# Low-rank rows by plain transfers, shared-expert matmuls in pieces of 5, 1, 1 and 5 pairs, expert rows summed tile by tile

## The reference

```python
def holo_linear(x, basis, phase, amp):          # basis 32x256, phase and amp 256x32
    resonance = jnp.einsum('bli,hi->blh', x, basis)
    w = amp * jnp.cos(phase)
    return jnp.einsum('blh,oh->blo', resonance, w)
# attention: 16 heads of 16
q, k, v = (split_heads(holo_linear(x, ...)) for each)
attn = jax.nn.softmax(jnp.einsum('bhqd,bhkd->bhqk', q, k) * scale, axis=-1)
out = holo_linear(join_heads(attn @ v), basis_o, phase_o, amp_o)
# experts: F = 352, best 2 of 8 by softmax of x @ gate_w.T, weights normed and times 2.5
g = silu(x @ w_gate[e]) * (x @ w_up[e]);  y = sum_e combine[t, e] * (g @ w_down[e])
shared = silu(x @ sw_gate) * (x @ sw_up) @ sw_down        # hidden size 704
return x + out(xn) + y(xn) + shared(xn)
```

## Time and profile before

| | |
|---|---|
| median of 3 runs | 1045.18 us (1043.41 to 1047.68) |
| the profiled execution | 1047.09 us, its span 1045.2 us |
| mean granted TensorE clock | 0.927 of full speed |
| PE busy | 888.3 us, 85% of the span |
| DVE busy | 642.8 us, 62% |
| ACT busy | 563.8 us, 54% |
| POOL busy | 328.7 us, 31% |
| 16 DMA engines, SyncE's queue | 42.2% |

### The profile page before, as it was taken

How to read it: one execution, slowest core, us unless ns; L and a number is a source line. 1 busy time by engine, 2 the same in 40 slices (tenths; PEclk the granted TensorE clock), 3 DMA queues, 4 the chain that set the end, 5 groups by cost and what they waited for, 6 DMA issues and landing times.

```text
span 1045.2 us, 19238 instructions
## 1 busy us (share of the span) xinstructions
PE 888.3 (85%) x6423; PEld 620.9 (59%) x6424; DVE 642.8 (62%) x978; ACT 563.8 (54%) x892; POOL 328.7 (31%) x305
## 2 busy tenths in 40 slices
PE   5646999999999956887997996996997998799988
PEld 3426999999999922445444554553644644545546
DVE  7767744444444373864784784785785686487653
ACT  4746644444444433663664664665565566466573
POOL 2004622222222031161261253234235126127235
PEclk9955999999999955998998998999999899899999
DMA  9974555222222143544654664664564575545220
GB/s 318 375 232 159 169 157 140 72 71 70 70 70 70 46 135 117 151 125 137 169 157 135 161 174 125 173 186 119 154 192 135 140 194 142 134 138 154 66 84 21
DMA packets 91537, 147.34 MB, mean 141 GB/s; under 512 B 17348, under 2 KB 51660, under 8 KB 88652
## 3 DMA queue, kind: packets, MB, share of 16 engines
q1 hardware_dynamic: 84780, 128.58, 42.2%
q0 software_dynamic: 6480, 17.70, 6.3%
q10 hardware_dynamic: 208, 0.14, 0.0%
HBM read 86.58 MB, written 54.71 MB: 135 GB/s over the span
## 4 chain that ended last, share of the span: by engine, by line
PE 54%; DVE 16%; DMA 15%; issue 6%; ACT 4%; POOL 2%; SPq 2%; POOLq 0%; DVEq 0%; ACTq 0%
DVE top L1836 8%; DMA r_v<-low_rank_rows 8%; PE bank L1266 7%; PE s_pair L1248 7%; PE st_pair L1248 6%; PE s_pair L1325 6%; DMA low_rank_rows<-r_lo 5%; PE bank L1409 5%; PE bank L1373 5%; PE bank L1483 4%; PE st_pair L1397 4%; ACT prob L1040 2%; PE bank L1256 2%; PE bank L1231 2%; PE bank L1423 1%
## 5 line engine op out<-in xcount | busy, mean ns | idle before, releaser
L1836 DVE TENSOR_REDUCE top<-s_pair 128x2 f32<-128x1024 f32 x252 | 308.3, 1224 | 198.1 <-PE s_pair L1325 197.2
L1040 ACT ACTIVATE prob<-st_pair 128x1024 f32<-128x1024 f32 x256 | 262.5, 1025 | 143.0 <-PE st_pair L1397 138.5
L751 POOL DMA_INDIRECT xg<-xn_rows,token_of x71 | 81.2, 1144 | 223.4 <-PE bank L1231 168.2
L784 POOL DMA_INDIRECT y_b<-expert_rows,slot_of x64 | 61.5, 961 | 265.7 <-PE st_pair L1397 260.6
L1325 PE MATMUL s_pair<-k_rows,q_rows 48*128 48x512 f32 x504 | 122.2, 478 | 24.6 <-DVE top L1836 23.2
L1373 PE MATMUL bank<-xT_b,w_sh 64*128 64x512 f32 x960 | 134.5, 397 | 4.9 <-DVE h_f L1857 3.5
L1397 PE MATMUL st_pair<-q_rows,k_rows 50*128 50x512 f32 x512 | 113.4, 437 | 18.4 <-ACT prob L1040 11.2
L1409 PE MATMUL bank<-prob,v_ones 128*32 128x512 f32 x1024 | 127.4, 616 | 0.0
L1373 PEld LDWEIGHTS bank<-xT_b,w_sh 64*128 64x128 f32 x960 | 89.8, 185 | 33.9 <-DVE h_f L1857 13.1
L1325 PEld LDWEIGHTS s_pair<-k_rows,q_rows 48*128 48x128 f32 x504 | 51.0, 196 | 76.4 <-DVE top L1836 59.7
L1266 PE MATMUL bank<-w_exp,c_hT 128*128 (+1 forms) x639 | 94.2, 292 | 1.0 <-ACT c_y L965 1.0
(11 more groups left out here) (233 smaller groups left out, 1109.9 us busy)
## 6 DMA issues: line engine op xcount, KB each, us to landing
xT_b<-xn_T_split SPq DMA_DIRECT2D x14, 1024.0 KB, 7.1
qk_rows<-qk_hi SPq DMA_DIRECT2D x56, 256.0 KB
q_rows<-qk_rows SPq DMA_DIRECT2D x64, 192.0 KB
k_rows<-qk_rows SPq DMA_DIRECT2D x56, 192.0 KB
expert_rows<-c_y SPq DMA_DIRECT2D x71, 128.0 KB, 1.7
xn_T_split<-x_T SPq DMA_DIRECT2D x8, 1024.0 KB, 6.5
qk_rows<-qk_lo SPq DMA_DIRECT2D x28, 256.0 KB
x_all<-in_L_attn_x_dram SPq DMA_DIRECT2D x8, 512.0 KB, 8.1
```

The costliest lines, as they stand in the source:

```text
L751: pool.indirect_dma_start(xg[s % 4][:, :], None, xn_dram, bass.IndirectOffsetOnAxis(token_of[:, s:s + 1], 0)).then_inc(c_x[s % 4], 16)
L784: pool.indirect_dma_start(y_b[:, t, k, :], None, y_dram, bass.IndirectOffsetOnAxis(slot_of[:, k, of(b) * TPB + t:of(b) * TPB + t + 1], 0)) ...
L1040: act.activation(prob[n % 3][:, 2 * jp:2 * jp + 2, :].rearrange("p j l -> p (j l)"), st_pair[:, :], ACT.Exp, scale=HD ** -0.5).then_inc(a_ ...
L1836: dve.tensor_reduce(top[g % 2][:, :, jp, qt], score_pair(b, g, v)[:, :].rearrange("p (i k) -> p i k", i=2), AX_X, ALU.max).then_inc(d_max, 1)
```

## The change

- The rows of q, k and v come into one buffer `r_rows[b % 2]` (96 partitions, 3 x 512), twice, in place of `r_qk` and two `r_v`. `load_low_rank` issues three transfers of 32 partitions each, HI, HI, LO, without a repeated source, in place of four. The wait for `b_qk` is one batch looser. `r_in` counts 48 a batch.
- To make room `r_lo` is the buffer `ro`; before ScalarE writes `ro` it waits for the stores of `r_lo`. An unused tile goes.
- SyncE issues `load_xT(b + 2)` in group 2 behind `load_max` and `load_rows`.
- The units of the shared expert are cut at 0, 5, 6, 7, 12 (down: 0, 10, 14, 19, 31, 34). Step 1 has the first piece, step 2 the second, then the small work, then the third, step 3 the fourth; down's fifth stays at the next step 0. The swap of the halves, with its wait for `b_ha`, lies between the second and the third piece.
- GpSimd scales and adds a tile's two expert rows as soon as its gathers and the one place later in its order allow (`sum_y`), with two semaphores `y_in`; `scale_y` and `add_pair` go. `hidden_low(b, 5)` is written at the head of the next batch's loop, where it stood at the end of its own.

```diff
             def load_low_rank(b):
                 wait(sp, r_st, (b + 1) * 32)
-                wait(sp, b_qk, b * 4)
+                wait(sp, b_qk, (b - 1) * 4)
                 wait(sp, b_v, (b - 1) * 2)
-                for rows, n, part in ((slice(0, 2 * HARM), 2, HI), (slice(2 * HARM, 3 * HARM), 1, LO)):
-                    src = r_dram[part].rearrange("(c h) n l -> c h (n l)", c=1).to_broadcast([n, HARM, 3 * L])
-                    sp.dma_start(r_qk[rows, :, :].rearrange("p n l -> p (n l)").bitcast(F32), src[:, :, 0:2 * L]).then_inc(r_in, 16)
-                    sp.dma_start(r_v[b % 2][rows, :].bitcast(F32), src[:, :, 2 * L:3 * L]).then_inc(r_in, 16)
+                for c, part in enumerate((HI, HI, LO)):
+                    sp.dma_start(r_rows[b % 2][c * HARM:(c + 1) * HARM, :, :].bitcast(F32), r_dram[part]).then_inc(r_in, 16)
...
-                if g == 2 and there(b + 2):
-                    load_xT(b + 2)
...
                 if there(rb):
                     load_rows(rb, rg)
+                if g == 2 and there(b + 2):
+                    load_xT(b + 2)
...
+            def sum_y(b, t):
+                wait(pool, y_in[t % 2], (b * 2 + t // 2 + 1) * 32)
+                for k in range(2):
+                    pool.tensor_scalar(y_b[:, t, k, :], y_b[:, t, k, :], share[:, of(b) * TPB + t, k:k + 1], None, ALU.mult).then_inc(p_ys, 1)
+                wait(pool, p_ys, (b * TPB + t + 1) * 2)
+                pool.tensor_tensor(y_b[:, t, 0, :], y_b[:, t, 0, :], y_b[:, t, 1, :], ALU.add).then_inc(p_yy, 1)
...
                 wait(act, b_po, b * 2)
+                wait(act, r_st, min(b + 3, NB) * 32)
                 act.activation(ro[:, :], res_bank(b)[0:96, :], ACT.Copy).then_inc(a_res, 1)
...
-            PIECES = ((0, 6), (6, 8), (8, 12))
-            DOWN_PIECES = ((0, 14), (14, 22), (22, 31), (31, 34))
+            CUTS = (0, 5, 6, 7, 12)
+            DOWN_CUTS = (0, 10, 14, 19, 31, 34)
...
-                    if t % 4:
-                        piece(b, g, t)
+                    if t % 4 == 1:
+                        piece(b, g, t, 0)
+                    if t % 4 == 2:
+                        piece(b, g, t, 1)
+                        small(b, g, t)
+                        piece(b, g, t, 2)
+                    if t % 4 == 3:
+                        piece(b, g, t, 3)
```

The order on GpSimd in a batch:

```diff
             for b in range(NB):
+                if there(b - 1):
+                    hidden_low(b - 1, 5)
                 gather_at(b, 0, 0, 4)
                 gather_at(b, 1, 0, 6)
                 gather_at(b, 2, 1, 0)
+                sum_y(b, 0)
                 gather_at(b, 3, 1, 2)
                 if there(b - 1):
                     ao_low(b - 1, 1)
                 hidden_low(b, 0)
                 gather_at(b, 4, 1, 7)
+                sum_y(b, 1)
                 gather_at(b, 5, 2, 1)
                 gather_at(b, 6, 2, 3)
                 hidden_low(b, 2)
                 gather_at(b, 7, 2, 6)
-                for n in range(4):
-                    scale_y(b, n)
+                sum_y(b, 2)
                 hidden_low(b, 3)
-                for n in range(4, 8):
-                    scale_y(b, n)
+                sum_y(b, 3)
                 ao_low(b, 0)
-                add_pair(b)
                 hidden_low(b, 4)
                 add_y(b)
-                hidden_low(b, 5)
+            hidden_low(LAST, 5)
```

More of the change, by code:

```diff
@@ L221, in build_program @@
         w_sh = sb("w_sh", [P, 2, S_ALL], F32R, late)
-        r_qk = sb("r_qk", [96, 2, L], F32R, late)
-        r_v = [None, sb("r_v1", [96, L], F32R, late)]
+        r_rows = [None, sb("r_rows1", [96, 3, L], F32R, late)]
         r_hi = sb("r_hi", [96, L], F32R, late)
-        r_lo = sb("r_lo", [96, L], F32R, late)
         qk_hi = [sb(f"qk_hi{i}", [P, L], F32R, late) for i in range(2)]
@@ L242, in build_program @@
         ro = sb("ro", [96, L], F32R, late)
+        r_lo = ro
         ao_T = sb("ao_T", [P, 2, KT, L], F32R, late)
@@ L247, in build_program @@
         o_b = sb("o_b", [P, TPB, D], F32, late)
+        r_rows[0] = sb("r_rows0", [96, 3, L], F32R, late)
         q_rows[0] = sb("q_rows0", [P, 2, L], F32R, late)
         k_rows[0] = sb("k_rows0", [P, 2, L], F32R, late)
-        r_v[0] = sb("r_v0", [96, L], F32R, late)
         xT_b = sb("xT_b", [P, 2, KT, L], F32R, late)
@@ L313, in build_program @@
         ob_in = sem("ob_in")
-        y_in = sem("y_in")
+        y_in = [sem(f"y_in{i}") for i in range(2)]
         m_in = [sem(f"m_in{i}") for i in range(2)]
@@ L554, in load_first_values @@
                 for c, part in enumerate((HI, HI, LO)):
-                    sp.dma_start(r_v[0][c * HARM:(c + 1) * HARM, :].bitcast(F32), r_dram[part, :, 2, :]).then_inc(r_in, 16)
+                    sp.dma_start(r_rows[0][c * HARM:(c + 1) * HARM, 2, :].bitcast(F32), r_dram[part, :, 2, :]).then_inc(r_in, 16)
             def store_y(s, i):
@@ L603, in store_low_rank @@
             def store_low_rank(b):
-                wait(sp, r_in, b * 64 - 16)
+                wait(sp, r_in, b * 48)
                 wait(sp, a_r, b + 1)
@@ L1314, in project @@
                     wait(pe, a_mt, (b - 1) * NG + 3)
-                pe.matmul(m_bank[:, :], w_rows[:, which, half * P:(half + 1) * P], r_qk[:, which, :], start=True, stop=True).then_inc(b_qk, 1)
+                pe.matmul(m_bank[:, :], w_rows[:, which, half * P:(half + 1) * P], r_rows[b % 2][:, which, :], start=True, stop=True).then_inc(b_qk, 1)
             def score(b, g, v):
@@ L1352, in gate_up_shared @@
                 f = ORDER[q]
-                first, end = PIECES[piece]
+                first, end = CUTS[piece:piece + 2]
                 if first == 0:
@@ L1463, in _ @@
             DOWN_ORDER = [(0, i) for i in range(FROM_LAST)] + [(1, i) for i in range(len(DOWNS))] + [(0, i) for i in range(FROM_LAST, len(DOWNS))]
-            assert (DOWN_PIECES[0][1], DOWN_PIECES[2][1]) == (FROM_LAST, FROM_LAST + len(DOWNS))
+            assert (DOWN_CUTS[2], DOWN_CUTS[4]) == (FROM_LAST, FROM_LAST + len(DOWNS))
             def down_pair(b, pair, piece):
-                first, end = DOWN_PIECES[piece]
+                first, end = DOWN_CUTS[piece:piece + 2]
                 if first == 0:
                     wait(pe, d_dn, b * TPB + 2) if pair else wait(pe, d_hf, b * SFT + SFT)
-                if piece in (1, 3):
-                    pe.wait_ge(b_ha, swaps(b, SFT + 2 * pair) + 1 + piece // 2)
+                if piece in (2, 4):
+                    pe.wait_ge(b_ha, swaps(b, SFT + 2 * pair) + piece // 2)
                 for m in range(first, end):
@@ L1542, in next_score, with piece @@
                     score(qb, qg, t - STEPS + AHEAD)
-            def piece(b, g, t):
-                what, c, j = unit(b, g, t // 4)
-                n = t % 4 - 1
-                if n < 0:
-                    what, c, j = unit_before(b, g, t // 4)
+            def piece(b, g, t, n):
+                what, c, j = unit(b, g, t // 4) if t % 4 else unit_before(b, g, t // 4)
+                if t % 4 == 0:
                     if what == "down":
-                        down_pair(c, j, 3)
+                        down_pair(c, j, 4)
                 elif what == "pair":
@@ L1557, in piece, with small @@
                         gate_up_both(c)
-                    if n == 2 and there(c - 1):
+                    if n == 3 and there(c - 1):
                         low_rank_o(c - 1)
+            def small(b, g, t):
+                if (g, t) in PROJECTED and there(b + 1):
+                    project(b + 1, PROJECTED.index((g, t)))
+                if g == 2 and there(b - 1):
+                    project_o(b - 1, t // 4)
+                if g == 3 and t == 2 and there(b + 2):
+                    low_rank(b + 2)
+                if g == 3 and t == 6 and there(b + 1):
+                    project_values(b + 1, 0)
             def slot(b, g):
@@ L1569, in slot @@
                         next_score(b, g, t)
[L1570 removed]
+                        piece(b, g, t, 4)
                     if t == 0 and there(pb):
```

29 lines of the change are left out of this document (6 added, 23 removed).

## The result

| | before, run beside it | after |
|---|---|---|
| median, us | 1045.77 | 987.57 (983.9 to 992.31, 4 runs) |
| ratio after / before | | 0.9447 (95% interval 0.9391 to 0.9503) |
| profiled execution; its span | 1047.09; 1045.2 | 992.31; 990.3 |
| granted clock, mean over the span | | 0.945 |

The forecast was 990 us (978 to 1012). The experiments are compared with that one. Where a price is given "by the ratios", it is the difference of two ratios times the 1044 us of the kernel before.

The account below looks back on a forecast made before the run. TensorE bounds the kernel outside its stalls, mostly waits for the low-rank load. From 1047.09 us: -52.4 - 3.5 + 2.4 + 0.7 - 3.0 - 0.3 = -56.1, 991.0; forecast 990 us, range 978 to 1012.

Parts of the forecast that it names:

- The stall and its price: TensorE's projection waits for the low-rank load at six batch changes; plain loads remove it whole, 8.74 us each, -52.4 us.
- The reading of the earlier trace as two engines: Low-rank loads with a source repeated twice run on two DMA engines, 0.13 of 16, about 50 GB/s; plain loads are freed.
- the load is no faster: Rival: traffic, not the source's shape, makes the low-rank load slow, so the stalls stay; 1051 us, chance 0.07.
- The start: Start of the attention part: 5.27 us stall gone, less 2.7 for later `xT_b`, 1 more granted; -3.5 us (0 to -8).
- `xT_b` behind the maxima: SyncE's queue, group 2: `xT_b` lands up to 1.5 us late for TensorE, 0.4 taken six times; +2.4 us (0 to +9).
- a half group outside the old stall that becomes longer: Sign against the prediction: if the batch outside the old stall lengthens, the pieces' order costs what was taken as hidden.
- The pieces: Shared expert's new cuts: moved matmuls fill TensorE's wait for exponentials, may lengthen that for maxima; -3 us (-10 to +8).
- The expert rows: GpSimd's tile-by-tile sums: no wait at the path within a batch, only the end gains; -0.3 us (0 to -1).
- SyncE's reserve: SyncE's store of new q/k rows loses the stall as reserve, but they are read a group later; nothing charged.
- The second buffer: `r_lo` sharing `ro`: ScalarE's added wait is for stores 30 us earlier, and the looser `b_qk` wait ended before; 0.
- The bare waits in the last batch: Last batch has no small work to hide the wait between pieces, six half groups; +0.7 us in all (0 to +2.5).
- more than forecast: Case where the steps' gaps close (-10) and the clock stays up from the start (-8): 977 us, chance 0.05.

Follow-up runs that it names:

- a_again: The kernel after, unchanged, measured once more with five executions: 986.16 us, ratio 0.9454 to the kernel before.
- b_wide_store: Kernel after with `xT_b` again loaded ahead of maxima and rows, and low-rank rows stored as 96 rows in partition order: 968.12 us, ratio 0.9271.
- c_wide_old_gpsimd: `b_wide_store` with GpSimd's scalings and sums in the order of the kernel before: 969.5 us, ratio 0.9288.

## Why the prediction held, step by step

**The stall and its price: right.** It went whole, and the plain loads alone do it. Forecast 52.4 us for six; measured 54.1. The projection has no wait in any batch. A load lands 3.6 us after its issue in the median (`a_again`), where I had 3.7 to 4.5. There is no half-clock stretch after the projection either: in the nine us from the head of a batch on, in all six changes of batch, the granted clock is 1.00 where the earlier trace rows had 0.88 and 0.50. The last of them (the projection is at 838.23):
```profile
833.00:842.00 9.00, 8.87 (x105) 6.18 (x101) 7.01 (x10) 5.95 (x8) 1.35 (x2) 1.00 0.71 206
```
Ahead of the heads it isn't always so (last section).
The reading of the earlier trace rows as two engines was right, and the reason drawn from it too. That the stores would stay on three engines was right too (0.19, above). The rival "the load is no faster" stood at 1051; two kernels that keep the two engines measured 1047.89 and 1054.94.

**The start: right in sum.** Forecast -3.5; the values matmuls half way through batch 0's group 0 stand at 398.66 after and 402.29 before, -3.6. The first `score_T` came 1.5 us later (388.39 against 386.92), where I had said 2 to 3.

**`xT_b` behind the maxima: the direct wait was sized rightly, the edit was not.** Forecast +2.4; the wait for `xT_b` is 2.9 us. But the edit costs 9.3 by the ratios, just past my upper bound of +9 (7.8 by the medians). The step that failed is the one that placed `xT_b` "behind max and rows" and counted only what it then waits for. I didn't go on down the same queue to what now stands behind *it*: `store_inverse`, one place further in the same slot, and through it `o_sum`, `ao`, `ro` and the maxima. I had watched for a half group outside the old stall that becomes longer, and it did, but I had laid it in advance on the pieces' order. The rule I had been working to, that each queue which a step is moved past counts, has a second half: who is now behind the moved step.

**The pieces: right sign, small.** Forecast -3 (-10 to +8), measured -5.1. The moved matmuls did fill the wait for the exponentials, by more than the third that I granted (9.6 to 2.9 us); the maxima's wait stayed where it was (13.5 and 14.3).

**The expert rows: wrong by about 4.** "Within a batch nobody waits for it at the path" is true of TensorE's table of waits, and not of the kernel: with the scalings back in group 3 the last half groups become longer. By what way is open. Charged -0.3, measured -4.0.

**SyncE's reserve: "nothing charged" was wrong for a neighbour.** I looked at the new q/k rows. It was the maxima's rows that lost the stall as their cover, 3.9 to 7.3 us with the plain loads alone (from 399 us on). With the whole change it is 2.4.

**The second buffer: charged 0, not tested.** No run takes back the second buffer, its looser wait for `b_qk` or the three issues in place of six by themselves.

**The bare waits in the last batch: not seen.** From the last batch's head to the end it is 83.04 us after and 83.95 before; I had charged +0.7.

Set beside the forecast's terms: -54.1 - 3.6 + 9.3 - 5.1 - 4.0 = -57.5, against 58.0 between the medians that `a_again` shares (1044.2 and 986.16). I forecast -56.1 with two errors, +7 too little for `xT_b` and -6 too little for pieces and GpSimd, which cancel. The total was right by its first term, 52 of the 56, and by luck in the rest.

That the measured terms sum so well is in part luck too, because they don't add up by another way. The plain loads alone bring 49 us and not 54.1 and 6.4, since they lose 8.4 elsewhere; the rest of the change brings 8.0 more (0.9531 to 0.9454), though its three tested parts, each undone by itself, sum to only +9.3 - 5.1 - 4.0 = +0.2. So some 8 us lie in how the parts work together, or in the second buffer and its three issues. Which of these it is stays open.

One sum in the prediction was off: with -10 for the pieces and -8 for the start in place of -3 and -3.5, "more than forecast" comes to 978.5 and not 977.

## What to carry to other kernels

Look at the outermost count of both sides of every transfer that someone waits for, after joining what is contiguous: 2 or 3 there meant two or three engines here, whether it came from a repeat, a padded layout or a `rearrange`, and a flat 0.13 or 0.19 in the windows gave it away. When a large transfer is moved in a queue, list what stands behind it in its new place, however small; a 16 KB store behind 1.8 MB was worth more here than the wait for the moved transfer itself. An idle second on one queue may be the cover of another wait: when a stall goes, read the next wait on the same queue first.

## What the runs showed of the hardware that was not expected

**The clock fell after short gaps too.** In the kernel after it isn't only the old stalls. Windows around 748 us, columns as in the earlier trace rows:
```profile
744.00:748.00 4.00, 4.00 (x32) 2.22 (x34) 1.58 (x3) 2.69 (x4) 2.56 (x3) 1.00 0.43 133
748.00:752.00 4.00, 2.44 (x21) 0.63 (x13) 3.67 (x6) 1.85 (x4) 1.27 (x1) 1.00 0.33 111
752.00:756.00 4.00, 3.91 (x20) 2.81 (x20) 2.39 (x3) 2.11 (x3) 2.84 (x2) 0.60 0.75 212
756.00:760.00 4.00, 4.00 (x22) 3.10 (x21) 1.23 (x1) 1.67 (x3) 0.75 (x1) 0.54 0.81 198
```
TensorE was busy 2.44 of 4 us, in pieces, at 1.00; then come two windows whose mean is 0.60 and 0.54, so by an estimate from these means nearly 7 us at 0.50, the lower level (1.2 GHz), with the engine full. That last half group is 12.79 us long, and the five others are 9.91 to 10.87. In this trace a second slow half group, of 13.25 us and with 0.50 from 866 to 872, stands in the last batch but one. In `a_again` there is one of 11.68, in another batch: TensorE is busy 2.28 of the 4 us from 674 to 678, and the clock is 0.78 and 0.50 in the two windows of 2 us from 676 on. That this makes the scatter between a kernel's own runs is likely and wasn't tested. `b_wide_store` has one (a half group of 11.81), and `c_wide_old_gpsimd` none behind its first batch.

**A store that can't be joined was issued more slowly.** SyncE takes 0.70 to 0.76 us for a store of 3 sets (192 KB), 0.32 for the same bytes as 96 rows, and the nine 64 KB loads take 0.74 each at the start with the sets 17 apart (6.70 us) and 0.57 with 16 (5.13 us).
